# Two mixture stages on one core: the first expert layer issued a whole token tile ahead of the second

## The reference, cut to what matters

```python
shared = relu(xt @ sW1 + sb1) @ sW2 + sb2
probs  = softmax(xt @ router_W + router_b)
top_p, top_i = top_k(probs, 3)
cw     = zeros((n, 15)).at[arange(n)[:, None], top_i].set(top_p)
h      = relu(einsum('nd,edh->neh', xt, eW1) + eb1)
ye     = einsum('neh,ehd->ned', h, eW2) + eb2
out    = shared + einsum('ned,ne->nd', ye, cw)
```

## Time and profile before, and how to read it

| what | value |
|---|---|
| runs of the kernel before | 3210.7, 3211.24 and 3217.59 us, median 3211.24 |
| span of the profiled execution | 3211.1 us |
| TensorE busy, whole span | 3002.0 us (93%) |
| VectorE, ScalarE, GpSimd busy | 2536.5, 2251.8, 1974.9 us |
| f1 in the span | 2471.8 to about 2743 us |
| f2 in the span | about 2933 to 3211 us |

### The profile page before, as it was taken

One profiled execution on the slowest core, in us unless ns is written; L12 is line 12 of the kernel. 1 busy time (PEld: TensorE's weight loads), 2 busy tenths in 40 slices (PEclk: granted clock), 3 DMA queues, 4 the chain that ended last, 5 costly groups with the idle time before them and its releaser, 6 DMA issues. The chain is left out here.

```text
span 3211.1 us, 83441 instructions
## 1 busy us (share of the span) xinstructions
PE 3002.0 (93%) x27212; PEld 2361.5 (74%) x27212; DVE 2536.5 (79%) x5859; ACT 2251.8 (70%) x6953; POOL 1974.9 (62%) x3125
## 2 busy tenths in 40 slices
PE   5569999999999999999999999999997999767999
PEld 3458888888888888888888888888876444455444
DVE  5669999999999999999999999999754454594554
ACT  4768888888888888888888888888643343412443
POOL 1588888888888888888888888888831000100000
PEclk8879999999999999999999999999998899957999
DMA  5457776767677766767777767677532332002322
GB/s 108 120 153 174 188 186 169 181 173 179 172 188 180 174 177 180 175 174 182 184 182 173 179 175 177 175 183 178 151 93 73 149 134 114 10 3 77 149 113 112
DMA packets 588205, 482.87 MB, mean 150 GB/s; under 512 B 464785, under 2 KB 504369, under 8 KB 581633
## 3 DMA queue, kind: packets, MB, share of 16 engines
q1 hardware_dynamic: 579328, 474.39, 55.8%
q10 hardware_dynamic: 8448, 3.15, 0.4%
HBM read 285.53 MB, written 191.86 MB: 149 GB/s over the span
## 5 line engine op out<-in xcount | busy, mean ns | idle before, releaser
L931 DVE SCALAR_TENSOR_TENSOR conv_k<-PP,tk,conv_k 128x256 f32<-128x256 f32 x1536 | 722.7, 479 | 61.8 <-ACT conv_k L766 33.6
L704 POOL TENSOR_TENSOR X<-X,tmp 96x31 f32<-96x31 f32 (+15 forms) x992 | 535.5, 540 | 77.7
L931 DVE SCALAR_TENSOR_TENSOR conv_v<-PP,tv,conv_v 128x256 f32<-128x256 f32 x1152 | 538.9, 477 | 44.9 <-ACT conv_v L766 35.3
L701 POOL TENSOR_TENSOR tmp<-At,X 96x31 f32<-96x31 f32 (+15 forms) x992 | 487.9, 492 | 63.1 <-DMA At<-n_d 4.9
L1100 PE MATMUL PP<-xn,wk 128*128 128x268 f32 x1024 | 341.9, 418 | 42.1 <-DVE conv_k L931 31.1
L687 POOL TENSOR_TENSOR rk<-ss,half 96x8 f32<-96x8 f32 x128 | 209.3, 1635 | 172.5 <-DVE ss L899 172.5
L669 POOL TENSOR_TENSOR Sg<-S,gend 128x512 f32<-128x512 f32 x256 | 266.8, 1042 | 60.4 <-DVE S L890 60.4
L738 ACT ACTIVATE recA<-TG,es 96x128 f32<-96x128 f32 x1024 | 285.4, 369 | 6.0 <-DVE es L924 6.0
L766 ACT ACTIVATE conv_k<-PP,tk 128x256 f32<-128x256 f32 x512 | 245.7, 482 | 58.7 <-PE PP L1100 51.9
L730 ACT ACTIVATE recA<-TG 128x128 f32<-128x128 f32 x1024 | 266.3, 273 | 24.2 <-PE TG L1151 24.2
L1064 PE MATMUL RB<-rhs,Yf 96*96 96x128 f32 x2048 | 269.0, 274 | 14.4 <-DVE rhs L879 14.4
(11 more groups left out here) (289 smaller groups left out, 6764.7 us busy)
## 6 DMA issues: line engine op xcount, KB each, us to landing
kqg_d<-kqgA SPq DMA_DIRECT2D x128, 512.0 KB, 6.1
kqgB<-kqg_d SPq DMA_DIRECT2D x128, 512.0 KB, 4.4
rec_d<-recA SPq DMA_DIRECT2D x128, 480.0 KB, 3.3
recB<-rec_d SPq DMA_DIRECT2D x128, 480.0 KB, 5.8
f1gates<-f1gates_d SPq DMA_DIRECT2D x24, 1024.0 KB, 6.6
f2gates<-f2gates_d SPq DMA_DIRECT2D x24, 1024.0 KB, 6.8
gdec<-gdec_d SPq DMA_DIRECT2D x128, 128.0 KB, 5.5
apk_d<-apkA SPq DMA_DIRECT2D x128, 128.0 KB, 3.3
```

What stands on the lines that cost most here:

```text
L701: nc.gpsimd.tensor_tensor(t, At[q % 2][:, j, j + 1:].unsqueeze(2).broadcast_to(sh), X[q % 2][:, j, 0:cols].unsqueeze(1).broadcast_to(sh), ...
L704: nc.gpsimd.tensor_tensor(x, x, t, ALU.subtract).then_inc(sub_ev, 1)
L931: return nc.vector.scalar_tensor_tensor(acc, src[:, :, j:j + SPAN], w[:, j:j + 1], acc, ALU.mult, ALU.add)
```

## The change

The lead of the first layer over the second becomes a whole tile: `LEAD = 16` instead of 2. TensorE issues `hidden(0, 0)` to `hidden(0, 2)`, then `r_ct(0)`, then `hidden(0, 3)` to `hidden(0, 15)`, and only then enters the loop, in which `hidden(n, e + 16)`, the same expert of the next tile, stands before the second-layer product of expert `e`. In the last tile no first-layer product is left. `hr` gets 16 places (`NE`), one per expert, so a rectification of tile `n` waits for the scaling of the same expert in tile `n - 1`. `hs` keeps 4 places.

ScalarE's side work is numbered anew, because its loop over tiles now runs a tile ahead of the second layer: `r_exp(n)` after expert 2, `square(n + 1)` after 5, `keep_xn(n + 1)` after 11, none of it in the loop's tile 0, and `keep_out(n - 2)` after 15, with one more `keep_out` behind the loop. One `Exp` of a single column (`warm`) is put at the head of ScalarE's program. In f2 `rows_of(n)` gets a wait for the output copy of tile `n - 4`, and `store_turn` waits for one more `keep_xn`.

```diff
+    LEAD = E_N + 1
-        hr, hs = sb("hr", [128, DEEP, TILE]), sb("hs", [128, DEEP, TILE])
+        hr, hs = sb("hr", [128, NE, TILE]), sb("hs", [128, DEEP, TILE])
+        warm = sb("warm", [128, 1])
...
+                if last:
+                    need(pe, st_ev, n - 4)
...
             def store_turn(n):
                 pe.wait_ge(acc_ev, n + 1)
-                pe.wait_ge(xn_ev, min(n + 3, NT))
+                pe.wait_ge(xn_ev, min(n + 4, NT))
...
-                if n == NT:
+                if n >= NT:
                     return
...
-            hidden(0, 0)
-            hidden(0, 1)
+            for e in range(WIDE):
+                hidden(0, e)
             r_ct(0)
+            for e in range(WIDE, LEAD):
+                hidden(0, e)
             pe.wait_ge(w2_in, 64)
...
-                    hidden(n, e + 2)
+                    hidden(n, e + LEAD)
...
+            nc.scalar.activation(warm[:, :], g.ident[:, 0:1], ACT.Exp)
             square(0)
...
                     act.wait_ge(h_mm[e], n + 1)
-                    if e >= DEEP:
-                        act.wait_ge(hs_ev[e - DEEP], n + 1)
-                    else:
-                        need(act, hs_ev[NE + e - DEEP], n - 1)
-                    nc.scalar.activation(hr[:, e % DEEP, :], ph[(n * NE + e) % WIDE][:, :], ACT.Relu, bias=b1[:, e:e + 1]).then_inc(relu[e], 1)
-                    if n + 1 < NT:
-                        if e == 3:
-                            r_exp(n + 1)
-                    if e == 6:
-                        square(n + 2)
-                    if e == 13:
-                        keep_xn(n + 2)
-                    if last and n and e == 15:
-                        keep_out(n - 1)
+                    need(act, hs_ev[e], n - 1)
+                    nc.scalar.activation(hr[:, e, :], ph[(n * NE + e) % WIDE][:, :], ACT.Relu, bias=b1[:, e:e + 1]).then_inc(relu[e], 1)
+                    if n:
+                        if e == 2:
+                            r_exp(n)
+                        if e == 5:
+                            square(n + 1)
+                        if e == 11:
+                            keep_xn(n + 1)
+                    if last and n > 1 and e == 15:
+                        keep_out(n - 2)
             if last:
+                keep_out(NT - 2)
                 keep_out(NT - 1)
...
-                        nc.vector.tensor_tensor(hs[:, e % DEEP, :], gates[n % 2][:, e, :], hr[:, e % DEEP, :], ALU.mult).then_inc(hs_ev[e], 1)
+                        nc.vector.tensor_tensor(hs[:, e % DEEP, :], gates[n % 2][:, e, :], hr[:, e, :], ALU.mult).then_inc(hs_ev[e], 1)
                     else:
-                        nc.vector.tensor_copy(hs[:, e % DEEP, :], hr[:, e % DEEP, :]).then_inc(hs_ev[e], 1)
+                        nc.vector.tensor_copy(hs[:, e % DEEP, :], hr[:, e, :]).then_inc(hs_ev[e], 1)
```

## The result

| | before | after |
|---|---|---|
| median of 4 runs each | 3210.97 us | 3189.04 us |
| lowest and highest | 3210.51 and 3217.59 | 3186.49 and 3192.42 |
| ratio, with its 95% interval | | 0.9925 [0.9911, 0.994] |
| span of the profiled execution | 3211.1 us | 3184.4 us |
| first row transposes to the start of the last `add`, f1 | 269.26 us | 258.30 us |

The kernel got faster. The medians differ by 21.9 us, and the ratio makes it 24.1 us of 3211 (19 to 29); forecast were 18.9. The profiled execution of after took 3186.49 us, 2.1 us of it outside its span. Its span is 26.7 us shorter than the span of before, of which 3.5 us lie in the stage ahead of f1, which the change doesn't touch; over all profiled executions here f1 begins anywhere from 2468.3 to 2476.5 us. The mixtures themselves, in the last two lines of the table, give -10.96 and -12.64, together -23.6 us.

The account below looks back on a forecast made before the run. TensorE's work was taken to bound the middle, so only the mixtures' heads could win: f1 -9.37 and f2 -9.51, together -18.9 us, 3211.2 to 3192.3 us (chance 0.66). The range was 3184 to 3202 us.

Parts of the forecast that it names:

- if the clock rises 8.75 us behind the first product: Head of each mixture: full clock comes 8.75 us after the first first-layer product, the mean of 8.94 and 8.57.
- the work balance behind the entry: Entering its loop, the new kernel stands where the old one stands 5.46 us later, in each mixture.
- (b): Rival, heads: the clock rises earlier, full from the first product; -27.6 us, 3183.6 us; chance 0.06.
- Third product and early Exp: Heads: router weights ready 1.29 us earlier, TensorE reaches r_ct 0.37 us later without waiting; nothing in the sum.
- Broadcast: Head of f1: comes 0.37 us later, first scaled expert from 2495.54, some 5 us before the loop wants it.
- rival (c): Loop's entry: no change, the burst's lead is given back because the broadcast ends last; 3211 us; chance 0.09.
- ScalarE in the burst: Heads: a rectification takes 0.686 us against 0.86 for the fastest product, so ScalarE stays hidden.
- The middle: Tiles behind the heads: work per tile is the same, scaling stays hidden, no gain counted.
- Rival (e): Middle gets faster: weight loads at 47% would leave room, the whole shrinking to about 2960 us; chance 0.01.
- rival (d): At var_eps between experts 7 and 8: VectorE's wait for squares becomes TensorE's, slower, 3218 us; chance 0.05.
- The clock's bounds: Heads: limits on the gain from when the clock rises, 12.9 us if late, 27.6 us if early.
- (a): Rival, heads: the clock comes later, counted from behind r_ct; -12.9 us, 3198.3 us; chance 0.13.

Follow-up runs that it names:

- e4: Changed kernel with the router-weight transposes r_ct(0) behind all 16 first-layer products instead of behind the third; 3209.7 us, ratio 0.9988 to the kernel before.
- e7: Changed kernel with a lead of 11 instead of 16, ScalarE's side jobs moved to match; 3189.35 us, ratio 0.9925 to the kernel before.
- e2: Changed kernel without the early Exp (warm); 3190.65 us, ratio 0.9928 to the kernel before.
- e1: Kernel before with only the early Exp added at the head of each mixture, lead still 2; 3208.42 us, ratio 0.9987 to the kernel before.
- e3: Changed kernel with a lead of 8 instead of 16, ScalarE's side jobs moved to match; 3196.04 us, ratio 0.9943 to the kernel before.
- after_again: The changed kernel, unaltered, measured once more as yardstick beside the second group of experiments; 3188.91 us, ratio 0.9924 to the kernel before.
- e6: Changed kernel with square(n + 1) after rectification 7 instead of 5; 3198.28 us, ratio 0.9951 to the kernel before.
- e9: Kernel of e3 with two useless products added in tile 0 before the first second-layer product; 3193.38 us, ratio 0.9932 to the kernel before.
- e5: Changed kernel with useless products ahead of the first norm transposes, two in f1, four in f2; 3188.0 us, ratio 0.9915 to the kernel before.
- e8: Changed kernel with useless products, three in f1, five in f2 ahead of the first norm transposes, one more behind them; 3185.39 us, ratio 0.9909 to the kernel before.

## Why the prediction was right, and where it was off

Its **reason held**: only the heads could win, by work that needs no router weights, put beside the broadcast. Shown by e4 (same products, broadcast behind them: gain gone), e7 (five fewer products ahead: gain whole) and e2 (early `Exp` out: gain whole but for some 1 us in f2).

**The step that failed is a size**: "if the clock rises 8.75 us behind the first product". It measured 4.95 us in f1 and 1.82 us in f2. The loop's entry lies at 16 x 0.86 + 0.44 = 14.20 us plus half of the slow time: with 8.75 that was the forecast's 18.54; with 4.95 it gives 16.7 (16.74 measured) and with 1.82 it gives 15.1 (15.18). This step is off by -1.80 - 3.36 = -5.16 us. What is then left of the measured lengths is the work balance behind the entry: forecast as -5.46 a mixture, it is -5.25 and -5.23, +0.44 in all, so the balance held to 0.23 us a mixture. -18.88 - 5.16 + 0.44 = -23.60 us, the sum of the two mixtures in the traces. That the time still fell inside the range is no merit of this step: the range reaches as far as (b), full clock from the first product.

The 8.75 us came from two dense runs behind a wait, 8.94 and 8.57 us. Other runs behind a wait show that even there it is no fixed delay. In f1 of e1 the rise came 8.1 us behind the first product after the wait (a mean of 0.80 over 2501 to 2502 puts it at 2501.40) and in f1 of e4 8.0 us, but in f2 of e1 6.26 and in f2 of e4 9.53, and in e3 7.1 us in both.

Behind the first product of a head it was never so late: in the eight profiles of the new order without useless products ahead (after, after_again, e2, e3, e4, e6, e7, e9) the rise came 1.7 to 2.2 us behind it in f2 and 1.8 to 5.0 us in f1. In f1 of e6, for one, it came 1.78 us behind a first product at 2482.72:

```profile
2484.00:2485.00 1.00, 1.00 (x3) 0.33 (x2) 0.85 (x8) 0.27 (x1) 0.00 (x0) 0.75 0.00 0
```

That TensorE has been busy at a head with transposes and logits already (4.48 us from the first of them to the first product in f1, above) may be why it is earlier than behind a wait; this was only argued, and it can't be all, since these 4.48 us are the same in after and in e6, with 4.95 and 1.78 us to the rise. Why f1 varies and f2 doesn't stays open. The Trainium skill (TensorE: Matmul & The Clock Gate, Part 1) says that the number of slow products at a start differs between runs of the same kernel; f1's 4.95 and 2.72 us in two executions of this one agree.

The other steps, one by one:

- *Third product and early Exp*: that TensorE would not wait for the weights was right. In f1 they came 1.42 us earlier against the first product (forecast 1.29), and TensorE reached `r_ct` 0.28 us later than before (0.37). In f2, with its early clock, it reached `r_ct` 1.27 us sooner than before (3.49 us behind the first product instead of 4.76), and there the early `Exp` is worth up to 1.3 us (e2), which the forecast put at nothing.
- *Broadcast*: in f1 the first scaling starts 6.45 us before its result is wanted, so rival (c) is out in this order. It is real at a lead of 8 (e3), and with `r_ct` last (e4).
- *ScalarE in the burst*: hidden, with 0.17 us to spare at each product at full clock.
- *The middle*: 20.00 of 20 us, products 0.86 us apart. Rival (e) fell: weight loads are busy 9.41 of 20 us there, still 47%, and with a lead of 16 the middle got no shorter. The Trainium skill (Perfetto Trace Analysis, "Identifying the Most-Contended Engine") judges TensorE by MFU, which was not worked out here, and by the busy share of weight loads; by that share there would have been room, and the 0.86 us a product show none.
- *The wait for the squares*, rival (d): the margin was put at 5.6 - 2.6 = 3.0 us and is 2.66 by e6. The mechanism is real: in e6 TensorE pays what goes beyond it in each of the tiles that have the step (six waits in each mixture).
- *The clock's bounds*: (a) fell. (b), full clock from the first product, 27.6 us, is what f2 nearly did; the result lies halfway between it and the forecast.

## What to carry to other kernels

Where a latency chain (router, DMA, broadcast) stands at a stage's head, start the chain first and put beside it just as much work as it takes, from whatever doesn't need it; more lead than that buys nothing. Price a pause of TensorE not by its length alone but, where the clock falls, with the slow work behind it, and count the margin of each in-order wait in the pace of the engine that mustn't stop, since a side job moved by two steps took two fifths of the gain back (9.4 of some 24 us). A clock delay measured behind a pause did not carry over to a start without one.

## What the hardware showed that was not expected

- A pause of 1.48 us at full clock brought half clock for 6.8 us and cost 3.4 us beyond itself (e3); filled with useless products it cost their 1.7 us and no more (e9). Two pauses of 1.02 and 0.78 us were followed by a fall as well (e5, f1), while one of 1.18 us in f2 of e2 stood among products at 1.00 without one. What tells these apart was not tried.
- The same kernel's f1 kept half clock for 4.95 us of products in one execution and for 2.72 in another, which is 1.1 us of its time. Over eight profiles whose heads are ordered alike ahead of that rise, f1 lies anywhere from 1.8 to 5.0 us and f2 within 1.7 to 2.2.
- Useless products paid: four in f1 and six in f2 made the mixtures 2.3 and 1.8 us shorter (e8).
